# Scan stage of a state-space block: the chunk's residual and norm moved from VectorE to TensorE and ScalarE

## The reference

```
xn = layernorm(x) * ln_w + ln_b
xi, z = split(xn @ W_in);  u = silu(causal_conv(xi))
dt_r, Bm, Cm = split(u @ W_xproj);  delta = softplus(dt_r @ W_dt + b_dt)
h[t] = h[t-1] * exp(delta[t] * A) + (delta[t] * u[t]) * Bm[t]     # 256 channels x 64 states
y[t] = sum over states of h[t] * Cm[t]
out  = ((y + u * D) * silu(z)) @ W_out
attn = x + out                     # the block's own residual
x1   = layernorm(x + attn)         # so the norm is of 2 * x + out
```

## Time and profile before

| | |
|---|---|
| time of the profiled execution | 2264.66 us |
| its span, first to last instruction | 2262.8 us |
| VectorE (DVE) busy | 1841.2 us, 81% of the span |
| ScalarE (ACT) busy | 1598.0 us, 71% |
| TensorE (PE) busy | 2139.4 us, 95% (matmuls' ends are modelled) |
| GpSimd (POOL) busy | 944.1 us, 42% |
| mean granted TensorE clock | 0.978 |
| 512 scans on VectorE (L1518) | 1157.1 us, 2310 ns each |

### The profile page before, as it was taken

How to read it: one execution, slowest core, us unless ns; L and a number is a source line. 1 busy time by engine, 2 the same in 40 slices (tenths; PEclk the granted TensorE clock), 3 DMA queues, 4 the chain that set the end, 5 groups by cost and what they waited for, 6 DMA issues and landing times. The chain is left out here.

```text
span 2262.8 us, 50361 instructions
## 1 busy us (share of the span) xinstructions
PE 2139.4 (95%) x16960; PEld 1260.6 (56%) x16960; DVE 1841.2 (81%) x2779; ACT 1598.0 (71%) x2070; POOL 944.1 (42%) x452
## 2 busy tenths in 40 slices
PE   7887999999999999999999997999999999999997
PEld 3342333333333333333333335899999999999986
DVE  5768999999999999999999997565565566556665
ACT  4677988888888888888888884555455455544543
POOL 3225343434444443434343443544444444444442
PEclk9895999999999999999999999999999999999999
DMA  5887222222221212122221225100100010000000
GB/s 166 249 242 190 44 45 44 46 41 45 42 46 39 46 39 46 39 49 42 46 45 41 47 47 149 38 0 0 38 1 0 0 38 1 0 1 1 10 10 18
DMA packets 354957, 114.93 MB, mean 51 GB/s; under 512 B 283000, under 2 KB 345600, under 8 KB 354624
## 3 DMA queue, kind: packets, MB, share of 16 engines
q1 hardware_dynamic: 350416, 110.92, 20.0%
q10 hardware_dynamic: 4464, 3.02, 0.4%
HBM read 67.98 MB, written 45.88 MB: 50 GB/s over the span
## 5 line engine op out<-in xcount | busy, mean ns | idle before, releaser
L1518 DVE TENSOR_TENSOR_SCAN arena<-behind 128x1040 f32<-128x1040 f32 x512 | 1157.1, 2310 | 6.9 <-ACT behind L961 4.3
L1062 ACT ACTIVATE arena<-PS,arena 128x512 f32<-128x512 f32 x512 | 343.1, 689 | 395.7 <-PE PS L1294 395.4
L951 ACT ACTIVATE behind<-PS 128x1024 f32<-128x1024 f32 x512 | 527.3, 1030 | 133.7 <-DVE arena L1518 101.3
L1197 PE MATMUL PS<-arena 128*32 128x128 f32 x8192 | 565.9, 406 | 0.0
L961 ACT ACTIVATE behind<-PS 128x1024 f32<-128x1024 f32 x512 | 539.2, 1053 | 7.4 <-PE PS L1180 3.8
L1306 PEld LDWEIGHTS PS<-arena 128*128 128x128 f32 x4096 | 476.3, 193 | 7.9
L1306 PE MATMUL PS<-arena 128*128 128x128 f32 x4096 | 476.6, 276 | 0.0
L771 POOL COPY behind<-carry 128x64 f32<-128x64 f32 x128 | 209.3, 1635 | 517.2 <-DVE arena L1518 382.1
L1294 PE MATMUL PS<-parts_xh,parts_w 128*128 128x512 f32 x1536 | 383.6, 401 | 14.4 <-ACT arena L1062 13.6
L1197 PEld LDWEIGHTS PS<-arena 128*32 128x32 f32 x8192 | 234.6, 119 | 287.7 <-issue 210.5
L1180 PE MATMUL PS<-arena 96*128 96x512 bf16 x1024 | 314.4, 389 | 53.0 <-ACT behind L961 38.7
(11 more groups left out here) (131 smaller groups left out, 1413.1 us busy)
## 6 DMA issues: line engine op xcount, KB each, us to landing
dl_d<-arena SPq DMA_DIRECT2D x48, 256.0 KB, 3.0
du_d<-arena SPq DMA_DIRECT2D x48, 256.0 KB, 3.3
arena<-dl_d SPq DMA_DIRECT2D x512, 24.0 KB
arena<-b_d SPq DMA_DIRECT2D x64, 192.0 KB
arena<-du_d SPq DMA_DIRECT2D x512, 24.0 KB
b_d<-arena SPq DMA_DIRECT2D x48, 128.0 KB, 2.8
u_d<-behind SPq DMA_DIRECT2D x8, 512.0 KB, 4.1
sz_d<-arena SPq DMA_DIRECT2D x8, 512.0 KB, 4.8
```

The costliest lines, as they stand in the source:

```text
L951: nc.scalar.activation(seg(dA[:, half])[:, :, 1:], PS[:, 0:2, :].rearrange("p j (i t) -> p (j i) t", t=TC), ACT.Exp).then_inc(exp_done, 1)
L1062: nc.scalar.activation(hT[:, e % 2, c], PS[:, HIDDEN[(GT * e + c) % 3], :], ACT.Gelu, bias=bias1[:, lp, e * GT + c:e * GT + c + 1]).then_i ...
L1197: last = nc.tensor.matmul(PS[32 * j:32 * j + 32, 4 + kk, 0:DB], cd[:, pair, j, 32 * i:32 * i + 32], seg(hb[kk])[:, :, 1 + 16 * j + i], sta ...
L1518: nc.vector.tensor_tensor_scan(hb[kk][:, q * QD * SEG:(q + 1) * QD * SEG], dA[:, q % 2], dB[:, G_, lo:lo + QD * SEG], 0.0, ALU.mult, ALU.a ...
```

## The change

TensorE's `project` gets two more matmuls per chunk, each with the identity matrix against `xres`, accumulated into the same PSUM region: they add x twice. VectorE's `add_residual` is gone for chunks 0 to 29, and `chunk_stats` reads PSUM directly. VectorE's `chunk_norm` is gone there too: ScalarE negates the mean (`negate_mean`, 128x1, block 1 iteration 0), subtracts it while reading PSUM (`centre`, 128x128, iteration 2), multiplies by 1/sqrt (`chunk_norm`, 128x128 from SBUF, iteration 4), and stores in iteration 5 instead of 3. `post_done`, on which SyncE's `load_post` waits, is now raised by ScalarE's multiplication. Chunks 30 and 31 (`in_end`) stay as they were.

```diff
@@
-        Q_EVACUATE, Q_TURN, Q_GATE, Q_PROJECT, Q_SUM, Q_STATS, Q_AGGREGATE, Q_NORM, Q_STORE, Q_CARRY = \
-            1, 6, 7, 3, 4, 5, 6, 2, 3, 3
+        Q_EVACUATE, Q_TURN, Q_GATE, Q_PROJECT, Q_STATS, Q_AGGREGATE, Q_NEGATE, Q_CENTRE, Q_NORM, Q_STORE, Q_CARRY = \
+            1, 6, 7, 3, 5, 6, 0, 2, 4, 5, 3
@@ ScalarE
+            def negate_mean(m):
+                act.wait_ge(p_var, m + 1)
+                apart(act)
+                nc.scalar.activation(nm_m[:], mv_m[:, 0, 0:1], ACT.Identity, scale=-1.0).then_inc(p_neg, 1)
+            def centre(m):
+                if held(m):
+                    act.wait_ge(x1_out, 16 * m)
+                act.wait_ge(p_neg, m + 1)
+                apart(act)
+                nc.scalar.activation(x1c, projected(m), ACT.Identity, bias=nm_m[:]).then_inc(p_centred, 1)
+            def chunk_norm(m):
+                act.wait_ge(p_centred, m + 1)
+                act.wait_ge(p_rs, m + 1)
+                apart(act)
+                nc.scalar.activation(x1c, x1c, ACT.Identity, scale=rs_m).then_inc(post_done, 1)
...
-                    if q == Q_STORE and kk == 1 and held(chunk - 1):
-                        store_x1(chunk - 2)
+                    if kk == 1 and held(chunk - 1):
+                        if q == Q_NEGATE:
+                            negate_mean(chunk - 2)
+                        if q == Q_CENTRE:
+                            centre(chunk - 2)
+                        if q == Q_NORM:
+                            chunk_norm(chunk - 2)
+                        if q == Q_STORE:
+                            store_x1(chunk - 2)
@@ TensorE
             def project(m):
                 pe.wait_ge(g_done, m + 1)
+                if held(m) and not (isinstance(m, int) and m == NCH - 1):
+                    pe.wait_ge(post_done, m)
                 for h in range(HALVES):
-                    last = nc.tensor.matmul(projected(m), G[:, h], wout_s[:, h], start=(h == 0), stop=(h == 1))
+                    last = nc.tensor.matmul(projected(m), G[:, h], wout_s[:, h], start=(h == 0),
+                                            stop=(h == 1 and in_end(m)))
+                if not in_end(m):
+                    for r in range(2):
+                        last = nc.tensor.matmul(projected(m), ident_s[:], xres, start=False, stop=(r == 1))
                 last.then_inc(out_ready, 1)
@@ VectorE
             def chunk_stats(m):
+                if in_end(m):
+                    dve.wait_ge(p_link, m * P_LINKS + 1)
+                    nc.vector.bn_stats(st_m[:, 0, :], xres_of(m)).then_inc(p_link, 1)
+                else:
+                    dve.wait_ge(out_ready, m + 1)
+                    nc.vector.bn_stats(st_m[:, 0, :], projected(m)).then_inc(p_link, P_LINKS)
...
                     if kk == 0 and held(chunk - 1):
-                        if q == Q_SUM:
-                            add_residual(chunk - 2)
                         if q == Q_STATS:
                             chunk_stats(chunk - 2)
                         if q == Q_AGGREGATE:
                             chunk_aggregate(chunk - 2)
-                    if q == Q_NORM and kk == 1 and held(chunk - 1):
-                        chunk_norm(chunk - 2)
```

More of the change, by code:

```diff
@@ L89, in build @@
         euler = sb("euler", [P, 1])
+        nm_m = sb("nm_m", [P, 1])
         ARENA = 39504
@@ L355, in build @@
         post_done = sem("post_done")
+        p_neg = sem("p_neg")
+        p_centred = sem("p_centred")
         f_g = sem("f_g")
@@ L479, in await_post, with in_end @@
                 eng.wait_ge(post_in, 80 * m + 80)
+        def in_end(m):
+            return isinstance(m, int) and m >= NCH - 2
         def turned(m, h):
@@ L1483, in chunk_stats @@
             def chunk_stats(m):
-                dve.wait_ge(p_link, m * P_LINKS + 1)
-                nc.vector.bn_stats(st_m[:, 0, :], xres_of(m)).then_inc(p_link, 1)
+                if in_end(m):
[4 more added lines that the diff above has]
+                    nc.vector.bn_stats(st_m[:, 0, :], projected(m)).then_inc(p_link, P_LINKS)
             def chunk_aggregate(m):
                 dve.wait_ge(p_link, m * P_LINKS + 2)
+                if held(m) and not (isinstance(m, int) and m == NCH - 1):
+                    dve.wait_ge(post_done, m)
                 apart(dve)
```

## The result

The changed kernel takes 2283.28 us (median of 6 runs, 2279.66 to 2284.65); the kernel before took 2265.78 us (median of 6, 2264.71 to 2272.36). The ratio is 1.0071, 95% interval 1.0058 to 1.0085: slower by 17.5 us, where 2256.5 us and a gain were forecast, with a range up to 2269.

What follows compares the result with a forecast made beforehand. The prediction took VectorE's list of instructions to bound the scan stage. From the profiled 2264.66 us, - 12.3 + 0 + 0 + 2.4 + 0.5 gave 2255.3, adjusted for run scatter to 2256.5 us, range 2251 to 2269.

Steps and rivals of the forecast that it cites:

- The residual and the norm, 12.3 us: VectorE in chunks 0 to 29: losing the residual (0.18 us) and norm (0.23 us) saves 30 x 0.41 = 12.3 us.
- Moments from PSUM at 0: VectorE's moments: reading PSUM instead of SBUF costs no more than the 0.19 us now, difference 0.
- ScalarE's three activations at 0: ScalarE: three small activations more a chunk, 0.35 us each, fit within the scans' pace and cost nothing.
- Project's extra 0.45 us at 0: TensorE's project: two more matmuls take 0.45 us; the delayed exponential's scan leaves 0.75 us, so nothing is lost.
- The late load, D = 0.98 us: SyncE's load of the next chunk, freed by the later norm, lands late; TensorE's turn is delayed by D = 0.98 us.
- Who waits for TensorE, 0.04 us a chunk: Behind turn: the exponential moves to 935.98, its scan loses 0.04 us; 0.08 a chunk taken in all, 2.4 us.
- The 0.5 us for the last chunk: Last chunk: the same late turn, with TensorE packed behind it and the final state sum waiting, costs 0.5 us once.
- waits of the scans over 8 us: VectorE's scans: the forecast counts as wrong if their waits sum to over 8 us.
- Rival 1: Late load: D 0.3 to 0.5 us larger, VectorE waits 9 to 15 us, time 2262 to 2269; chance 0.25.
- Rival 2: ScalarE's multiplication slips behind iteration 5's exponential and copy, D 3.2, time 2320, half a slip 2287; chance 0.07.
- Rival 3: Turn: no stall at all, D below 0.94, time 2252.4 or 2253.6 us; chance 0.16.
- Rival 4: ScalarE becomes the bound in three iterations with a new activation, 9.9 us back, time 2262.3; chance 0.10.

Runs made afterwards that it cites:

- e1: Changed kernel, but SyncE's load of the next chunk's u, silu(z) and x waits for project (`out_ready`) instead of the norm (`post_done`): 2257.39 us, ratio 0.9962.
- e7: Kernel before with the norm alone moved to ScalarE, at early iterations, subtracting from `xres`; residual and moments stay on VectorE: 2262.15 us, ratio 0.9986.
- e5: Changed kernel with only the residual moved: ScalarE's three steps out, VectorE norms from PSUM in block 1 iteration 2: 2263.03 us, ratio 0.9991.
- e2: Changed kernel with ScalarE's steps earlier: negation block 0 iteration 7, subtraction block 1 iteration 0, multiplication 2, store 3: 2256.19 us, ratio 0.9962.
- e4: Kernel before with two more float32 matmuls of 128x128 in front of each turn, 0.45 us more of TensorE there: 2279.70 us, ratio 1.0059.
- e6: Changed kernel with turn in iteration 7 of block 1, behind its products and arguments, and gate in the next block 0, iteration 0: 2260.27 us, ratio 0.9976.

## Why the prediction was wrong

- *VectorE sets the stage, and only what delays a scan counts*: right. In e1, the scans wait as little as before. "VectorE never waits" was too strong: the scans that open a block or a group of four follow a copy of ScalarE at a fixed distance, as the next point and the failed step show.
- *The residual and the norm, 12.3 us*: too high. With the stalls gone (e1) the stage is 9.5 us shorter (1105.74 - 1096.23). The rows of single scans show that some of the norm's 0.23 us comes back. The two scans of iterations 3 and 4 of block 1 (the second opens a group of four), with ScalarE's copy of iteration 3, in the kernel before, behind the norm, and in e1, behind a scan:

```profile
923.43 4.53 DVE L1518 TENSOR_TENSOR_SCAN arena<-behind 128x1040 f32<-128x1040 f32 x2
...
924.32 1.05 ACT L961 ACTIVATE behind<-PS 128x1024 f32<-128x1024 f32 x1
```

```profile
956.12 4.62 DVE L1565 TENSOR_TENSOR_SCAN arena<-behind 128x1040 f32<-128x1040 f32 x2
...
957.24 1.05 ACT L968 ACTIVATE behind<-PS 128x1024 f32<-128x1024 f32 x1
```

  The pair takes 4.62 us instead of 4.53. So a removed small step was worth less than its own distance to the next scan: e7 gives (1105.74 - 1100.80) / 30 = 0.16 us for the norm. The second scan needs the copy of iteration 3: before, the scan (925.67) came 0.30 us behind the copy's end, and in e1 (958.41) 0.12 us. The same 0.12 us stands in front of the scan of iteration 4 of block 0 in both kernels, so the copy is the likely limit here too; no run tests it. The residual gave 9.5 - 4.9 = 4.6 us instead of 5.4. The scan at the start of block 1 follows its predecessor by 2.36 us in e1 (947.09 to 949.45) and by 2.32 before (914.21 to 916.53); e5 has this too, and e7 has not.
- *Moments from PSUM at 0*: right, 0.19 us from either. The Trainium skill's figures (VectorE: DVE Perf Modes, section "The TRN2 errata — SBUF-src ops pay a fixed extra latency per instruction") would make it 65 ns more, an estimate. The trace disagrees for the moments, and agrees for the norm from PSUM in e5, 0.07 us more.
- *ScalarE's three activations at 0*: right (e1 and e2). The subtraction took 0.37 us, and still only 0.36 from its start to the next exponential. *Project's extra 0.45 us at 0*: right, but for at most the 0.04 us at the start of block 1 just named, which the runs do not divide between the missing residual and the longer project.
- *The late load, D = 0.98 us*: right on the average. The multiplication ended 939.49, and the last issue came 2.58 us later (2.52 in the prediction). In the 28 waits, turn's weight load stood idle for 31.4 / 28 = 1.12 us; 0.12 us stands there before too, so turn was 1.0 us late. In the chunk shown it came 944.25 - 943.17 = 1.08 us behind the arguments, where before it came 931.91 - 931.68 = 0.23 us behind them: 0.85 us late. The products behind turn came 945.24 - 943.17 = 2.07 us behind the arguments instead of 1.34: 0.73 us late, for TensorE made up 0.12 us in turn.
- *Who waits for TensorE, 0.04 us a chunk*: this is the step that failed. It followed the delay to the exponential at 935.23, whose scan is the one after next and had 1.0 us. It passed over the copy of the products between turn and that exponential, which the scan behind `gate` waits for at the block's start. That copy ended 934.72, the scan started 935.01, and the 0.29 us between them recur in the changed kernel (0.28), in e4 (0.28) and in e6 (0.29): the slack was 0. So whatever the products behind turn are late reaches VectorE: 0.73 us in the chunk shown, and the scan came 1.21 - 0.48 = 0.73 us later behind `gate`. With e1 as what the kernel would be without the stall, it cost 26.4 us, 0.88 a chunk, where 2.4 us were summed.
- The sum as measured: - 9.5 + 26.4 = + 16.9 us in the stage, with 17.5 us between the medians. The 0.5 us for the last chunk is shown apart by no run. The prediction's own sign for being wrong, waits of the scans over 8 us, came true with 31.3 us.
- Rival 1 had the mechanism, with a D that would have to grow; D did not grow, the slack was smaller. The price was beyond its 15 us, and the scan that waited was the one right behind `gate`, not the one after it. Rival 2 is out, for the multiplication stands right behind its copy (939.10). Rival 3 is out, for turn stalled. Rival 4 is out, for e1 keeps ScalarE's three activations, and its scans wait as little as before.

The fastest versions are e1 and e2, both with a ratio of 0.9962, 0.38% under the kernel before.

## What to carry to other kernels

When a step is moved later, find every instruction that waits for what it frees, and for the first delayed engine check each of its results by its own deadline: the tightest was not the next one that was visibly waiting, but an intermediate copy whose lateness a small step on the bound engine had just hidden. A start that keeps the same distance to a producer's end while everything else around it moves (0.28 to 0.29 us here, in four kernels) is a sign of a bound with no slack, also where the trace shows no idle time; a test like e4 or e6 confirms it. Free a buffer when its last reader is done, not when the whole item is.

## What the runs showed of the hardware

- From the end of ScalarE's copy to the start of the scan at a block's start there were 0.28 to 0.29 us in the chunks shown of four kernels. In the next chunk it was 0.22 (before: 971.62 to 971.84) and 0.23 (changed kernel, below), and the two distances alternate from chunk to chunk. In the middle of a block it was 0.12. From the end of the same copy to TensorE's next weight load there were 0.05 us (before, the copy at 926.79 ended at 927.84, and the next products' weight load began at 927.89). The scan stands behind five waits at a block's start, of which the one for the copy is the first, and behind three in the middle; that these make the difference is argued, not tested.

```profile
983.38 1.06 ACT L968 ACTIVATE behind<-PS 128x1024 f32<-128x1024 f32 x1 [1.04 <-PE PS L1215]
...
984.67 2.36 DVE L1565 TENSOR_TENSOR_SCAN arena<-behind 128x1040 f32<-128x1040 f32 x1 [0.87 <-ACT behind L968]
```

- An activation of 128x128 with the mean as bias, from PSUM, took 0.37 us (L1000), one without it 0.28 us (L979). Both rows of the changed kernel:

```profile
934.67 0.37 ACT L1000 ACTIVATE arena<-PS,nm_m 128x128 f32<-128x128 f32 x1
...
951.52 0.28 ACT L979 ACTIVATE arena<-PS 128x128 f32<-128x128 f32 x1
```

- VectorE's subtract-and-multiply of 128x128 took 0.32 us from SBUF and 0.38 from PSUM, while its moments took 0.27 from either.
